# Running counts of two bucket sorts taken in eight pieces through PSUM, and an earlier buffer release by GpSimd

## The reference

```python
edge_index = jnp.stack([src, dst])
x = _layernorm(x + _L0_gnn_ref(x, src, dst, edge_weight, L0_gnn_weight), axis=-1)
x = _layernorm(x + _L1_gnn_ref(x, ..., edge_index), axis=-1)
x = _layernorm(x + _L2_gnn_ref(x, edge_index, ...), axis=-1)
x = _layernorm(x + _L3_gnn_ref(x, edge_attr_32, src, dst, ...), axis=-1)
```

## Time and profile before

| what | us |
|---|---|
| median of 3 runs | 41089.48 (41085.13 to 41089.79) |
| the profiled execution's span | 43473.8 |
| first sort, 843 to 3789 us of the span | 2946 |
| of it DVE, PE, POOL busy | 794.6, 729.5, 2218.0 |
| second sort, 3789 to 6795 us | 3006 |
| of it DVE, PE, POOL busy | 796.2, 729.6, 2218.3 |
| layers up to 20000 us | 13205 |
| from 20000 us to the end | 23474 |

### The profile page before, as it was taken

The page is one execution under the profiler, slowest core; times in us unless marked ns, Lnnn a source line. Parts: engine busy times, 40 slices in busy tenths (PEclk is TensorE's granted clock), DMA queues, the critical chain, the costliest instruction groups (busy, mean ns, idle before and its releaser), DMA issues. The chain is left out here.

```text
span 43473.8 us, 513712 instructions
## 1 busy us (share of the span) xinstructions
PE 30181.7 (69%) x99425; PEld 18063.7 (42%) x99426; DVE 28834.6 (66%) x61982; ACT 11318.1 (26%) x26426; POOL 32170.2 (74%) x31499
## 2 busy tenths in 40 slices
PE   5222223444447322228999999999999999999999
PEld 5222222333347222224444444444444444444444
DVE  6222222222127322228999999999999999999999
ACT  0000000111111000003444444444444444444444
POOL 1777775555540565667998999899889989998997
PEclk8555555665555555559999999999999999999999
DMA  1111001221121001002111111111111111111111
GB/s 44 35 34 27 17 17 46 61 60 23 21 45 56 14 12 12 12 12 43 46 46 44 46 46 46 43 47 46 43 47 46 46 43 46 46 46 44 46 46 42
DMA packets 1365766, 1669.90 MB, mean 38 GB/s; under 512 B 847196, under 2 KB 1012047, under 8 KB 1252303
## 3 DMA queue, kind: packets, MB, share of 16 engines
q1 hardware_dynamic: 664232, 1115.69, 8.0%
q0 software_dynamic: 669696, 495.09, 7.6%
q10 hardware_dynamic: 31680, 57.69, 0.4%
HBM read 1393.98 MB, written 274.47 MB: 38 GB/s over the span
## 5 line engine op out<-in xcount | busy, mean ns | idle before, releaser
L1695 PE MATMUL l3m_p_w<-en,l3m_hid 128*128 128x512 f32 x42240 | 20968.5, 619 | 648.5 <-issue 257.1
L1745 DVE TENSOR_REDUCE l3m_xg<-l3m_prod 128x32 f32<-128x1024 f32 x10560 | 12851.0, 1217 | 190.3 <-POOL l3m_prod L1626 0.2
L1617 POOL DMA_INDIRECT l3m_xg<-wide_table,l3m_mt x10560 | 10340.5, 979 | 2390.5 <-issue 2148.6
L1626 POOL TENSOR_TENSOR l3m_prod<-l3m_rest,l3m_xg 128x384 f32<-128x384 f32 x10560 | 10675.1, 1011 | 279.5 <-ACT l3m_rest L1672 93.6
L1695 PEld LDWEIGHTS l3m_p_w<-en,l3m_hid 128*128 128x128 f32 x42240 | 7165.7, 189 | 6865.1 <-issue 5413.8
L1672 ACT COPY l3m_rest<-l3m_p_w 128x384 f32<-128x384 f32 x10560 | 5050.4, 478 | 12814.3 <-PE l3m_p_w L1695 11849.2
L1757 DVE TENSOR_TENSOR l3m_prod<-l3m_p_w,l3m_xg 128x512 f32<-128x512 f32 x10560 | 7186.3, 681 | 420.5 <-PE l3m_p_w L1695 232.6
L1707 PEld LDWEIGHTS l3m_p_sum<-l3m_xg,l3m_apart 128*125 128x125 f32 x21120 | 3965.3, 188 | 5090.4 <-issue 2739.7
L1660 ACT ACTIVATE l3m_apart<-iota_lo,l3m_mt 128x125 f32<-128x125 f32 x10560 | 4238.5, 402 | 0.7 <-DMA l3m_mt<-dst_meta 0.7
L1707 PE MATMUL l3m_p_sum<-l3m_xg,l3m_apart 128*125 128x64 f32 x21120 | 3474.1, 246 | 22.8 <-DVE l3m_xg L1745 22.8
L849 POOL DMA_INDIRECT l2a_xg<-table,l2a_mt x1760 | 1676.2, 952 | 2441.7 <-DMA l2a_mt<-dst_meta 1886.1
(11 more groups left out here) (324 smaller groups left out, 22212.1 us busy)
## 6 DMA issues: line engine op xcount, KB each, us to landing
l3m_hid<-hid_t SPq DMA_DIRECT2D x660, 1024.0 KB
l3m_xg<-wide_table,l3m_mt POOLq DMA_INDIRECT x10560
hid_t<-l_hid SPq DMA_DIRECT2D x110, 1024.0 KB, 4.1
order_src_bk<-dst_bucket SPq DMA_DIRECT2D x52, 808.0 KB
order_dst_bk<-src_bucket SPq DMA_DIRECT2D x52, 808.0 KB
by_dst<-order_src_empty SPq DMA_DIRECT2D x28, 1071.0 KB, 24.5
l_rec<-by_dst SPq DMA_DIRECT2D x110, 272.0 KB, 3.7
l_xg<-table,l_mt POOLq DMA_INDIRECT x1760
```

Of the source, the lines that this page charges most:

```text
L1617: pool.indirect_dma_start(xg[s][:, j, 0:2 * D], None, wide_table[:, :], bass.IndirectOffsetOnAxis(ap=mt[s][:, j, 0:1].bitcast(I32), axis=0 ...
L1626: pool.tensor_tensor(o_i(prod[j % RING][:, OWN:HD]), o_i(rest[j % RING][:, :]), state_of(s, j, REST), ALU.mult).then_inc(pooled, 1)
L1695: ins = pe.matmul(p_w[j % 2][:, c * 512:(c + 1) * 512], hid[s][:, j * P:(j + 1) * P], en2[:, c * 512:(c + 1) * 512], start=True, stop=True)
L1745: dve.tensor_reduce(xg[s][:, j, 2 * D:3 * D], o_i(prod[j % RING][:, :]), AX, ALU.add).then_inc(msgs, 1)
```

## The change

The scan and the product are done in eight pieces of 512 columns. A scan writes its piece into one of two PSUM tiles, and begins from the last column of the piece before (or from `carry`). Its second tensor operand is no longer `hit` but one column of zeros in PSUM, broadcast; the result, the larger of the running sum and that operand, stays the running sum. The product takes the piece from PSUM and writes `count` in SBUF. The copy to `carry` comes after the last product and after the signal `placed`. GpSimd's wait for the chunk before and its increment of `free` move from behind the 32nd scatter to behind the 8th.

```diff
             K = NB + 1
+            EARLY, PIECE = 8, 512
...
                 p_pos = ph.ps("p_pos", [P, 512])
+                p_zero = ph.ps("p_zero", [P, 512])
+                p_run = [ph.ps(f"p_run{s}", [P, PIECE]) for s in range(2)]
...
                         dve.memset(empty[:, :, :], 0.0)
+                        dve.memset(p_zero[:, :], 0.0)
...
-                                dve.tensor_tensor_scan(count[0:K, :], hit[0:K, :], hit[0:K, :], carry[0:K, :],
-                                                       ALU.add, ALU.max)
-                                dve.drain()
-                                dve.tensor_copy(carry[0:K, :], count[0:K, CHUNK - 1:CHUNK])
-                                dve.drain()
-                                dve.tensor_tensor(count[0:K, :], count[0:K, :], hit[0:K, :],
-                                                  ALU.mult).then_inc(placed, 1)
+                                for n in range(CHUNK // PIECE):
+                                    cols = slice(n * PIECE, (n + 1) * PIECE)
+                                    run = p_run[n % 2]
+                                    begin = p_run[(n + 1) % 2][0:K, PIECE - 1:PIECE] if n else carry[0:K, :]
+                                    dve.tensor_tensor_scan(run[0:K, :], hit[0:K, cols],
+                                                           p_zero[0:K, 0:1].broadcast_to([K, PIECE]), begin,
+                                                           ALU.add, ALU.max)
+                                    dve.drain()
+                                    ins = dve.tensor_tensor(count[0:K, cols], run[0:K, :], hit[0:K, cols], ALU.mult)
+                                ins.then_inc(placed, 1)
+                                dve.tensor_copy(carry[0:K, :], run[0:K, PIECE - 1:PIECE])
                                 dve.drain()
...
                             for t in range(CC):
                                 pool.indirect_dma_start(rows, bass.IndirectOffsetOnAxis(ap=idx[s][:, t:t + 1], axis=0),
                                                         rec[s][:, t, :], None).then_inc(sent[s], 16)
-                            if not first:
-
-                                pool.wait_ge(sent[1 - s], (i + s) * (16 * CC))
-                                pool.sem_inc(free, 1)
+                                if t == EARLY - 1 and not first:
+
+                                    pool.wait_ge(sent[1 - s], (i + s) * (16 * CC))
+                                    pool.sem_inc(free, 1)
```

## The result

| kernel | median us | ratio to before (95% interval) |
|---|---|---|
| before | 41,089.6 | |
| changed | 40,622.7 | 0.9885 (0.9874 to 0.9897) |

The change makes the kernel 467 us faster. I had forecast 1,315 us, with at least 760. The changed kernel's profiled execution has a span of 40,607.7 us, in step with its runs. The one profile that I had of the kernel before was not: 43,473.8 us, where its runs take 41,090.

A forecast was written before the change was run, and what follows sets the result against it. Key loading was taken to bound the sorts at about 56 us a chunk; 41.5 after saves 1,519 us of profile. Gains of 1,436 (scaled) or 1,193 off 41,089.5 give 39,654 or 39,896; middle 39,775, range 39,470 to 40,330.

The forecast's parts named there:

- nothing else is edited: Only the two sorts, about 2,940 and 3,000 us of the 43,473.8 us span, were taken as touched by the change.
- No change: something outside these loops: Rival: something such as key loads at an unseen rate holds the unprofiled sorts; time 41,090 us, chance 0.03.
- GpSimd still blocked: Rival: DVE operations still hold up GpSimd's scatters, so 52.7 us a chunk remains; time 40,733 us, chance 0.06.
- GpSimd's 41.0 us a chunk: Sorts, after the change: 32 scatters at 1.262 us plus 0.57 us still lost to the comparison L428.
- All three lie at 41: Sorts: GpSimd 41.0, DVE with TensorE 40.9, key loading 40.6 us a chunk; with mutual waits, 41.5 was taken.
- The pieces: Sorts, DVE: eight scans of 1.29 us and eight products of 0.680 us, 2.05 us a piece, 16.4 us in all.
- Scan dear in PSUM: Rival: a piece costs 3 us instead of 2.05, DVE's loop 48.5 us; time 40,330 us, chance 0.08.
- the slower rival: Rival: a piece at 4.6 us makes DVE's serial loop 61.2 us a chunk; time 41,550 us, chance 0.03.
- Blocked scatters: Sorts: scatters lose 12.34 us a chunk to DVE operations; 8.23 (scan) and 3.53 (product) go, 0.57 (comparison) stays.
- The load loop: Sorts: key load to buffer release, closing over two chunks: 112.7 us before, 81.2 after, so 40.6 a chunk.
- L442's wait: Sorts: DVE's wait for TensorE's L460 products, 14.12 us with GpSimd idle, 22.30 with scatters throughout; expected near 22.
- in the profiled execution alone: Case: L442 waits beyond 14 us exist only under that profile; unprofiled sorts already run at 52.7, gain 1,193 us.

The follow-up runs named there:

- the kernel before, again: The kernel before, unedited, run and profiled a second time: 41,080 us, with a profiled span of 41,078.3 us.

## Why the prediction was wrong, step by step

- **The step that failed** is in the first paragraph: "nothing else is edited". I read it as "no other stage changes", and gave neither the 82 added instructions nor the place of later loops a cost, a rival or a look. It cost 746 us and took the result out of the range (39,470 to 40,330; measured 40,623). Without it the kernel takes 39,875 us, 100 above the forecast of 39,775. "No change: something outside these loops" was a rival only for the sorts. The measured time lies 110 us from the 40,733 of "GpSimd still blocked", a rival that the sorts' rows refute; the time alone would have pointed to the wrong cause.
- **GpSimd's 41.0 us a chunk**: right. The period was 41.1 in both sorts, 0.4 below the 41.5 that I took for loops in each other's way. "All three lie at 41" was wrong: the wait for L460 is 14 us and DVE's loop 32, and the load loop has slack as well (below).
- **The pieces**: 1.29 + 0.69 with starts 1.97 apart; I had 2.05 a piece. From the comparison to the last product it is 17.2 us, 17.8 forecast. PSUM costs the scan nothing that shows, nor does the 1.0 us a chunk that I had estimated from the Trainium skill. "Scan dear in PSUM" and with it the slower rival fall.
- **Blocked scatters**: right in size: 8.23 and 3.53 go, 0.6 stays. The cause is shown for the scan; for the product it stays argued. "Never over 1.6 us" was missed: scatters that meet the comparison reach 1.91 (1.94 in the kernel before, again).
- **The early release**: right that its wait costs nothing. GpSimd waits for DVE once in the whole first sort, and the scatters follow each other after 0.30 us of issue.
- **The load loop**: the load took 36.8 and then 37.1 us in the first sort; right, and the run with 112 partitions shows that the number of rows made it slow. The sum for the loop after the change was not: its "about 1.5" stands for the way from L450 to `free`, for which the text before it has 1.05 and about 4. With these the sum is 84.7 us, or 42.4 a chunk, above GpSimd's 41.0. That the forecast did not suffer is luck: the "about 4" was too high. SP goes on 1.1 us after a chunk's first scatter (2026.99 to 2028.15 in the timeline above), and by the medians of the first sort the loop needs 1.1 + 1.9 + 37.1 + 31.9 + 1.05 = 73 us for two chunks, 36.5 each.
- **L442's wait**: I said it would be near 22, and it is 14.1. "With scatters all through it, 22.30" gave the scatters a part that they don't have. I took the middle between "everywhere" (1,436 us) and "in the profiled execution alone" (1,193). The second was nearly right: the undisturbed periods were 53.8 and 52.7, and the sorts gave 1,227. The forecast lies 100 us from the 39,875 of the change without the stall, and would have been 21 us from it by the second alone. The mark was in the table: an execution 5.8% above its runs. The rows called the release "remote", a writer that the profile doesn't name.
- **The chance of 0.94 for faster** held.

## What to carry to other kernels

A change that adds or removes instructions moves every loop behind it on that engine. Compare the packets of the instruction queue and the time of every untouched stage before judging an edit; where a stage that was not edited has changed, some idle instructions (64 and 174 here) ahead of its loop show whether it is the place. Two bounds close to each other hide each other's cure, so try the edits together and alone. And before summing on a profile, compare its span with the runs: here the one that stood 5.8% above them had waits that the runs didn't have.

## What the runs showed of the hardware

- A DVE loop of 301 instructions costs 4.7 us of standstill at each jump back in one place of the program and none in three others; TensorE's granted clock falls to the lower level with it, and the net price is 2.3 us of 69.4. Of the 4.7 us, 2.85 pass before the instruction packet starts, with the DMA engines full of a data load.
- A scan reading one tile from SBUF and one column from PSUM leaves GpSimd's indirect DMAs at 0.96 us for all of its 8.75 us; with two operands from SBUF a scatter took 9.19.
- A load of 101 rows of 8 KB took 34 to 37 us from its issue to the comparison, of 112 rows 5.1 (second sort) to 7.9 (first).
- GpSimd's queue takes instructions some twelve ahead of the engine: `free`, placed behind the 32nd scatter, was given while the twentieth ran.
